# Edge stages of a graph network: sums of edge weights and counts of edges from [weights, ones] as the stationary operand and a plain float32 one-hot as the moving one

## The reference, cut to what matters

```python
e_in = jnp.concatenate([x[row], x[col]], axis=-1)
ef = jax.nn.relu(e_in @ ei_w1 + ei_b1) @ ei_w2 + ei_b2
ew = jax.nn.sigmoid(ef @ ew_w + ew_b)[:, 0]
deg = jax.ops.segment_sum(ew, col, num_segments=N) + 1.0     # sums of weights
...                                                         # first graph convolution
cat = jnp.concatenate([out1[row], out1[col], ef], axis=-1)
ef = _layernorm(ef + (jax.nn.relu(cat @ eu_w1 + eu_b1) @ eu_w2 + eu_b2), lne_g, lne_b)
ew = jax.nn.sigmoid(ef @ ew_w + ew_b)[:, 0]                  # weights again, and deg again
...                                                         # second graph convolution
deg = jax.ops.segment_sum(jnp.ones_like(src), dst, num_segments=n)   # counts of edges
```

## Time and profile before

| | |
|---|---|
| median of 3 launches | 6701.0 us |
| lowest and highest | 6698.0 and 6709.4 us |
| span of the profiled launch | 6714.1 us |
| TensorE matmul busy | 4993.9 us (74%) |
| VectorE busy | 3976.5 us (59%) |
| ScalarE busy | 2624.4 us (39%) |
| GpSimd busy | 3591.2 us (53%) |
| first edge stage (first to last gather) | 157 to 2377 us |
| second edge stage (first to last gather) | 3171 to 5274 us |

### The profile page before, as it was taken

The page is one execution under the profiler, slowest core; times in us unless marked ns, Lnnn a source line. Parts: engine busy times, 40 slices in busy tenths (PEclk is TensorE's granted clock), DMA queues, the critical chain, the costliest instruction groups (busy, mean ns, idle before and its releaser), DMA issues. The chain is left out here.

```text
span 6714.1 us, 158802 instructions
## 1 busy us (share of the span) xinstructions
PE 4993.9 (74%) x41016; PEld 3317.3 (49%) x41016; DVE 3976.5 (59%) x16487; ACT 2624.4 (39%) x4173; POOL 3591.2 (53%) x4285
## 2 busy tenths in 40 slices
PE   2565566565566658885999999999999577767996
PEld 1222222222222236764666666666666366656885
DVE  4666666666666668885555545555554488883113
ACT  2444444444444435554333333334333255543001
POOL 2777777777777711112777777777777311141000
PEclk6777777777777767676999999999999767768998
DMA  4777777777777747774777777777777477743553
GB/s 110 199 204 199 201 201 199 199 201 201 199 203 200 201 126 220 221 219 123 222 221 219 219 217 220 221 219 221 220 219 220 116 212 220 223 132 138 183 183 124
DMA packets 1122380, 1308.17 MB, mean 195 GB/s; under 512 B 225167, under 2 KB 861175, under 8 KB 1121882
## 3 DMA queue, kind: packets, MB, share of 16 engines
q1 hardware_dynamic: 853994, 791.46, 39.1%
q0 software_dynamic: 155136, 423.83, 24.4%
q10 hardware_dynamic: 113184, 92.13, 5.1%
HBM read 972.33 MB, written 334.56 MB: 195 GB/s over the span
## 5 line engine op out<-in xcount | busy, mean ns | idle before, releaser
L816 POOL DMA_INDIRECT counts<-tab_p,idx x1616 | 1672.5, 1035 | 533.9 <-issue 492.8
L816 POOL DMA_INDIRECT counts<-tab_pr,idx x1616 | 1556.4, 963 | 534.3 <-issue 482.0
L1114 PE MATMUL pz<-tmpb,pieces 96*128 96x64 bf16 x1616 | 132.0, 212 | 965.8 <-DMA counts<-tab_p,idx 641.3
L1459 POOL TENSOR_TENSOR acc<-acc,pieces 128x32 f32 x808 | 200.4, 248 | 1117.9 <-ACT pieces L1336 1015.1
L929 DVE BATCH_NORM_STATS2 st<-pz 128x6 f32<-128x64 f32 x1616 | 252.8, 219 | 871.1 <-PE pz L1085 863.7
L1114 PEld LDWEIGHTS pz<-tmpb,pieces 96*128 96x128 bf16 x1616 | 87.6, 107 | 1203.5 <-issue 1203.0
L1084 PE MATMUL pz<-wz,pieces 96*128 96x65 f32 x3232 | 665.3, 289 | 0.8 <-ACT pieces L1205 0.8
L918 DVE TENSOR_SCALAR counts<-cell_ids,counts 128x950 bf16<-128x950 f16 x1616 | 650.8, 467 | 0.0
L1085 PE MATMUL pz<-wv,pieces 128*128 128x65 f32 x3232 | 644.9, 282 | 0.0
L1205 ACT ACTIVATE pieces<-pu,eub 128x512 f32<-128x512 f32 x404 | 277.8, 688 | 780.7 <-PE pu L1074 778.6
L1124 PE MATMUL pu<-counts,pieces 128*128 128x475 bf16 x1616 | 565.7, 517 | 10.0 <-DVE counts L918 9.9
(11 more groups left out here) (326 smaller groups left out, 8972.4 us busy)
## 6 DMA issues: line engine op xcount, KB each, us to landing
kept_d<-counts SPq DMA_DIRECT2D x808, 256.0 KB
counts<-kept_d SPq DMA_DIRECT2D x808, 256.0 KB
pieces<-rel_d SPq DMA_DIRECT2D x404, 192.0 KB
pieces<-rel_d ACTq DMA_DIRECT2D x404, 192.0 KB
counts<-counts_d SPq DMA_DIRECT2D x93, 698.2 KB, 7.4
counts<-srcp_d SPq DMA_DIRECT2D x808, 64.0 KB
counts_d<-tmpb SPq DMA_DIRECT2D x202, 232.8 KB
counts<-counts_d SPq DMA_DIRECT2D x31, 931.0 KB, 4.8
```

Source lines behind the costliest of these rows:

```text
L816: pool.indirect_dma_start(out=rows[:, par, u, j, 0:width], out_offset=None, in_=table, in_offset=bass.IndirectOffsetOnAxis(ap=idx[:, 2 * h ...
```

## The change

`hotd` and the multiplication that makes it go away, and with them the semaphore `s_hotd`. `hot` becomes float32 with a sub-tile's 32 window columns contiguous. `wts` gets a second column of ones for each column of edges. For each of the 16 columns of edges one product has the two columns [weights, ones] as its stationary operand and the 32 columns of `hot` as the moving one; the four groups' results stand in partitions 0, 32, 64 and 96 of `pd[0]` (two rows each: sum and count), so each group has another quarter of the array's columns. Both stages run these 16 float32 products, in place of four float32 ones (and four bf16 ones in the first stage) of 128 columns. PE waits for `hot` and for the sigmoid where it waited for `hotd`, and ACT waits with the next sigmoid for the products (`s_sum`) where it waited for `hotd`. The adds go to two rows in each group's quarter of `acc`, and each waits for the add of the same group an iteration ago, no longer for the add just before.

`acc` then holds four partial sums of each node's degree (and four partial counts); `degrees` stores and loads four rows in place of one, and DVE adds them with one more reduction for each of two or three layouts before ACT takes the root. All of `acc` is cleared in place of its first rows.

```diff
         hot_of(it):
-                            hot[:, :, :], iota_row[:, :].unsqueeze(2).broadcast_to([P, WIN, U * SUB]),
-                            rel[:, ds(it * U * SUB, U * SUB)].unsqueeze(1).broadcast_to([P, WIN, U * SUB]),
+                            hot[:, :, :], iota_row[:, :].unsqueeze(1).broadcast_to([P, U * SUB, WIN]),
+                            rel[:, ds(it * U * SUB, U * SUB)].unsqueeze(2).broadcast_to([P, U * SUB, WIN]),
                             ALU.is_equal).then_inc(s_hot, 1)
-                    def weigh_hot(it):
-                        dve.wait_ge(s_sig, done(it))
-                        dve.wait_ge(s_hot, done(it))
-                        nc.vector.tensor_tensor(hotd[:, :, :], hot[:, :, :],
-                                                wts[:, :].unsqueeze(1).broadcast_to([P, WIN, U * SUB]),
-                                                ALU.mult).then_inc(s_hotd, 1)
         add(it, u, first):
                         dve.wait_ge(s_sum, done(it))
-                        dve.wait_ge(s_acc, done(i - 1))
-                        sums = 1 if update else WIN + 1
-                        a = acc[0:sums, ds(first, WIN)]
-                        nc.vector.tensor_tensor(a, a, pd[0][0:sums, u * WIN:(u + 1) * WIN], ALU.add).then_inc(s_acc, 1)
+                        dve.wait_ge(s_acc, done(i - U))
+                        a = acc[u * WIN:u * WIN + 2, ds(first, WIN)]
+                        nc.vector.tensor_tensor(a, a, pd[0][u * WIN:u * WIN + 2, 0:WIN], ALU.add).then_inc(s_acc, 1)
         step (DVE):
-                            if behind > 0 and u == U - 1:
-                                weigh_hot(it - 1)
         degrees_of(it):
-                        pe.wait_ge(s_hotd, done(it))
+                        pe.wait_ge(s_hot, done(it))
+                        pe.wait_ge(s_sig, done(it))
                         pe.wait_ge(s_acc, done(it * U - 1))
-                        by_tile = lambda v: v.rearrange("p w (u j) -> p j u w", j=SUB)
-                        if not update:
-                            for j in range(SUB):
-                                nc.tensor.matmul(pd[0][WIN:WIN + 1, 0:U * WIN], ones_half[:, :],
-                                                 by_tile(hot)[:, j, :, :], start=(j == 0), stop=(j == SUB - 1))
                         for j in range(SUB):
-                            last = nc.tensor.matmul(pd[0][0:1, 0:U * WIN], ones_col[:, :],
-                                                    by_tile(hotd)[:, j, :, :], start=(j == 0), stop=(j == SUB - 1))
+                            for u in range(U):
+                                c = u * SUB + j
+                                last = nc.tensor.matmul(pd[0][u * WIN:u * WIN + 2, 0:WIN], wts[:, c, :], hot[:, c, :],
+                                                        start=(j == 0), stop=(j == SUB - 1))
                         last.then_inc(s_sum, 1)
         weights_of(it) (ACT):
-                        act.wait_ge(s_hotd, done(it - 1))
-                        nc.scalar.activation(wts[:, :], zl16[:, :], ACT.Sigmoid, bias=(zb if update else ewl)[:, 0:1],
+                        act.wait_ge(s_sum, done(it - 1))
+                        nc.scalar.activation(wts[:, :, 0], zl16[:, :], ACT.Sigmoid, bias=(zb if update else ewl)[:, 0:1],
         degrees(again):
-                    sp.dma_start(deg_d[0:1, :], acc[0:1, 0:NPAD]).then_inc(s_store, 16)
+                    sp.dma_start(deg_d[:, 0, :], acc[0:P:WIN, 0:NPAD]).then_inc(s_store, 16)
-                    for r_, d_ in ((0, dinv), (1, cinv))[0:1 if again else 2]:
-                        sp.dma_start(d_[:, :], deg_d[r_, :].rearrange("(p t) -> p t", t=NT)).then_inc(s_load, 16)
+                    for r_, d_ in ((0, deg_parts), (1, cnt_parts))[0:1 if again else 2]:
+                        sp.dma_start(d_[:, :, :], deg_d[:, r_, :].rearrange("u (p t) -> p u t", t=NT)).then_inc(s_load, 16)
...
+                    nc.vector.tensor_reduce(dinv[:, :], deg_parts[:, :, :].rearrange("p u t -> p t u"), axis=AXX,
+                                            op=ALU.add).then_inc(s_pe, 1)
+                    nc.vector.tensor_reduce(dinv_h, deg_parts_h.rearrange("p u t -> p t u"), axis=AXX,
+                                            op=ALU.add).then_inc(s_pe, 1)
+                    if not again:
+                        link(nc.vector.tensor_reduce(cinv[:, :], cnt_parts[:, :, :].rearrange("p u t -> p t u"), axis=AXX,
+                                                     op=ALU.add))
```

More of the change, by code:

```diff
@@ L74, in build @@
         base_d = dram("base_d", (G,), I32)
-        deg_d = dram("deg_d", (2, NPAD))
+        deg_d = dram("deg_d", (U, 2, NPAD))
         srcp_d = dram("srcp_d", (EPAD,), BF16)
@@ L122, in build @@
         assert spare <= 2 * NT * D + 2 * U * SUB * SW and 3 * HT % 2 == 0
-        TAIL = U * SUB * WIN * 3 // 2 + 2 * SUB * ED
+        TAIL = U * SUB * WIN + 2 * SUB * ED
         pieces = sb("pieces", [P, 3 * NT * D // 2 + TAIL])
@@ L159, in build @@
         o9 = 3 * NT * D // 2
-        hotd = pieces[:, o9:o9 + U * SUB * WIN].rearrange("p (w c) -> p w c", w=WIN)
+        hot = pieces[:, o9:o9 + U * SUB * WIN].rearrange("p (c w) -> p c w", w=WIN)
         o9 += U * SUB * WIN
-        hot = pieces[:, o9:o9 + U * SUB * WIN // 2].bitcast(BF16).rearrange("p (w c) -> p w c", w=WIN)
-        o9 += U * SUB * WIN // 2
         win = tmpb[:, 0:2 * U * D].rearrange("p (s u f) -> p s u f", s=2, u=U)
@@ L166, in build @@
         wu = sb("wu", [ED, D])
-        wts = sb("wts", [P, U * SUB])
-        ones_col = sb("ones_col", [P, 1])
-        ones_half = sb("ones_half", [P, 1], BF16)
+        wts = sb("wts", [P, U * SUB, 2])
+        deg_parts = sb("deg_parts", [P, U, NT])
+        cnt_parts = sb("cnt_parts", [P, U, NT])
         st16 = sb("st16", [P, U * SUB, 6])
@@ L328, in build @@
         s_batch = [sem(f"counts_loaded{b}") for b in range(2)]
-        all_sems = [s_load, s_store, s_pool, s_dve, s_act, s_pe, s_idx, *sum(s_gat, []), *sum(s_win, []), s_hotT, s_hot, s_hotd, s_t,
+        all_sems = [s_load, s_store, s_pool, s_dve, s_act, s_pe, s_idx, *sum(s_gat, []), *sum(s_win, []), s_hotT, s_hot, s_t,
                     s_relu, s_u, s_urelu, s_z, s_zcp, s_sum, s_acc, s_stage, s_sig, s_sqrt, s_kept,
@@ L612, in _ @@
                 nc.vector.memset(pq_bias[:, ED:2 * ED], 0.0).then_inc(s_bias, 1)
-                nc.vector.memset(ones_col[:, :], 1.0)
-                nc.vector.memset(ones_half[:, :], 1.0)
+                nc.vector.memset(wts[:, :, 1:2], 1.0)
                 nc.vector.memset(ones[:, :], 1.0)
@@ L743, in build, with reset_windows @@
         count_rounds = nc.values_load(rounds_sb[0:1, 3:4], min_val=1, max_val=CMAXR)
-        def reset_windows(clear_weights=False, clear_rows=0, clear_bank=None, cells=False):
+        def reset_windows(clear_weights=False, clear_rows=False, cells=False):
             with nc.Block() as block:
@@ L760, in _ @@
                         nc.vector.memset(ew[:, :], 0.0)
-                    if clear_bank is not None:
-                        nc.vector.memset(clear_bank[0:WIN + 1, 0:U * WIN], 0.0)
                     if clear_rows:
-                        nc.vector.memset(acc[0:clear_rows, :], 0.0)
+                        nc.vector.memset(acc[:, :], 0.0)
                     if cells:
@@ L1021, in step @@
                             variance(it)
-                    for s_ in (s_zcp, s_hot, s_hotd, s_kept, s_acc) + ((s_hotT,) if update else (s_t, s_relu, s_hit)):
+                    for s_ in (s_zcp, s_hot, s_kept, s_acc) + ((s_hotT,) if update else (s_t, s_relu, s_hit)):
                         dve.sem_inc(s_, CREDIT)
@@ L2202, in degrees @@
             loads = 48 if again else 64
+            deg_parts_h = pieces[:, 0:U * HT].rearrange("p (u t) -> p u t", u=U)
             with nc.Block() as block:
@@ L2236, in _ @@
                 def _(act):
-                    act.wait_ge(s_load, loads)
+                    act.wait_ge(s_pe, 2)
                     nc.scalar.activation(dinv[:, :], dinv[:, :], ACT.Sqrt, bias=1.0).then_inc(s_act, 1)
@@ L2248, in aggregate @@
                 sum_kept_round(x_again)
-        reset_windows(clear_weights=True, clear_rows=WIN + 1, clear_bank=pd[0], cells=True)
+        reset_windows(clear_weights=True, clear_rows=True, cells=True)
         with nc.Fori(0, rounds):
@@ L2254, in build @@
         finish_first()
-        reset_windows(clear_weights=True, clear_rows=1)
+        reset_windows(clear_weights=True, clear_rows=True)
         with nc.Fori(0, rounds):
```

10 lines of the change are left out of this document (4 added, 6 removed).

## The result

The changed kernel takes 6666.8 us in the median of 4 launches (6662.4 to 6672.9), the kernel before 6702.2 beside it; the ratio is 0.9947, 95% interval 0.9933 to 0.9961. Taken once more beside the experiments it was 6668.0 us and 0.9959 (0.9945 to 0.9973). The prediction was 6671 us, range 6648 to 6708.

What follows compares the result with a forecast made beforehand. GpSimd's gathers were taken to bound both edge stages. From the profiled 6714 us, -30 (held gathers), -6 (stage ends) and +6 (`degrees`) gave 6684; timed launches lie 13 lower, so 6671 us, range 6648 to 6708.

Steps and rivals of the forecast that it cites:

- Part 1: First edge stage: without DVE's multiplication (line 981) its holds of gathers go, -30 us (0 to 45); second stage 0.
- Rival (a): First stage: gathers fall at random on lines 914 and 918, so 15 of 30 us come back, 6686; chance 0.30.
- slope of 0.97: First stage's iterations compared: time grows 0.97 us for each us line 981 holds gathers, so little is made up elsewhere.
- Rival (c): Gathers' remaining holds fall too as the stage's rhythm loosens: twice the gain, 6641 us; chance 0.07.
- Part 2: DVE's line 973, making `hot` in float32, costs as much and holds gathers as before: 0.
- Part 3: PE's products, both stages: 32 passes take 1.1 us an iteration in place of 1.89; worth 0.
- rival (b): Second stage: PE becomes the bound at 3.3 us of products an iteration; at 4.3, 6772 us at most; chance 0.13.
- Part 4: New waits of PE for `hot` and sigmoid, and of sigmoid for products: costed at 0; uncovered, 111 us in first stage.
- Part 5: Ends of both stages after the last gather: no multiplication, quicker adds and products, -3 us each, -6 in all.
- Part 6: `degrees`: added reductions, +1.0 and +1.4 us, and more rows to load, 1.8 each call: +6 us (2 to 37).

Runs made afterwards that it cites:

- after_again: The changed kernel, unedited, measured once more beside the follow-up experiments: 6668.0 us, ratio 0.9959 to the kernel before.

## Why the prediction was right

- **The bound.** GpSimd's gathers set both edge stages, and the idle time in front of them is 534 us in every run in which the stages kept their length, those among them that gave PE or DVE work back.
- **Part 1**, -30 us: right in place, size and cause. Taking the multiplication alone away gave 29 us in the first stage and some 4 in the second, putting it back cost 25 to 33 in the first. The gain of the first profile, 40 (32 in `after_again`), has 5 us of gathers that are 3 ns shorter in the median; that median was 946 or 947 in the first stage of all but one of the kernels made from the changed one (949 with six wide products), and 949 in the two others. What makes these 3 ns stays open.
- **Rival (a)**, line 918 taking 15 us back: it went from 99 to 96 and line 914 from 15 to 13 (97 and 16 in `after_again`), so next to nothing came back. Its price was misread: the 114 us that the prediction set beside its 129 count waits twice. Counted once they are 92, and by the rival's sum all of the 30 us would have come back. The slope of 0.97 that stood against it has a standard error of 0.24 in that trace; it was the runs that settled this. Rival (c), remaining holds falling too: not by themselves, only when their inputs were moved.
- **Part 2**, 0: line 967 at 692 ns, and its holds as before, 11 us.
- **Part 3**, 0 by way of 1.1 us of products: the 0 holds, the term was mis-sized. The products take 0.41 to 0.61 us. The row it came from had 128 moving columns, four times as many, and the prediction called it an upper figure but used it. It made rival (b) look nearer than it was; its threshold of 3.3 us proved to be some 2.9. Rival (b)'s own price, 4.3 us without the change of the quarter, was further off: 0.76.
- **Part 4**, 0: right in size. The sigmoid made DVE late by 11.8 us in the first stage, and GpSimd not at all. That the wait for `s_sum` made the sigmoid late isn't shown: the run without the multiplication has that wait too, and there DVE never waits for the sigmoid in that place (22.4 us of idle time, as before).
- **Part 5**, -3 each: the first stage's end gained 4.2 us. Without the multiplication alone it gained 0.5, so it was the adds and products, not the instruction that the prediction named first. The second stage's end read -7.6, but in the runs with the same products it lies between 18.5 and 25 us, and in the run without the multiplication, which has the old products, at 20.7. So this end shows no size; that PE stands elsewhere in its iteration when the last gather ends wasn't tested.
- **Part 6**, +6: measured +8.3. The loads were the mis-sized term. From the store's issue to the landing are 10.0 us in the first call and 7.4 in the second; before, 6.4 and 5.1, so +3.6 and +2.3 in place of 1.8 each. The two reductions cost 1.24 us each time (1.4 and 1.0 predicted; the third one of the first call runs beside the root).
- **Sum.** -30 and -6 and +6 against -30, some -5 for the ends, +8 and some -5 for the shorter gathers: a sum of about -32 where -30 was forecast and the medians show -35 and -30; the second stage's -3 to -7 come on top. That the total fits so closely is in part luck: the shorter gathers, which the prediction didn't have, make up for the 2 us that `degrees` cost above the forecast.

## What to carry to other kernels

When GpSimd's gathers set the pace, look at their mean against their median, and lay every stretched one beside the VectorE instruction that ends with its hold: time removed from VectorE is worth nothing there, but each of its operations that holds gathers is worth the overlap that it causes: here those with two inputs in SBUF, and the comparisons of a row in SBUF with a scalar (line 912 here, line 904 in the earlier trace rows). Moving one input to an idle PSUM bank takes the hold away even where it makes the operation slower (467 to 705 ns, and 78 us gained). Count a wait beside two operations once. A cheaper product on an engine that isn't the bound gave nothing here; say by how much it would have to grow to become one, and test that with few wide instructions, not with many small ones.

## What the runs showed of the hardware

- A gather is held from about 0.13 us after its start until the VectorE instruction that runs then ends, plus its own 0.82 us, if that instruction is one that holds. Beside a multiplication with both inputs in SBUF: 1.35 us. With one in PSUM: 0.94, at the same 0.68 us of VectorE.
- The comparison of 950 float16 numbers takes 467 ns from SBUF and holds 78 us of gathers, each wait counted once; from PSUM 705 ns, holding 3.
- Float32 products of 2 stationary and 32 moving columns: passes start 7 ns apart where the column quarter changes each time, 18 ns where eight in a row use one. Loads run beside products in both orders.
- 384 such passes an iteration left TensorE standing inside them, in the iteration shown twice for 2.5 us, with no releaser shown; with 128 no gap was over 0.37 us. Behind that standing the granted clock was 0.50, the lower of two levels, for 9.4 us.
